# Attention scores of two heads in the two halves of TensorE: 64 rows for each head in place of 96 and 128 shared rows

## What is computed

```python
def attention(x):                       # x: 4 x 512 x 256
    q, k, v = split(x @ w_qkv.T + b_qkv)
    q, k = rope(q), rope(k)
    attn = einsum('bhqd,bhkd->bhqk', q, k) * 16 ** -0.5
    attn = softmax(where(causal, -inf, attn))
    return einsum('bhqk,bhkd->bhqd', attn, v) @ w_out.T + b_out

def ffn(x):
    hidden = silu(x @ W1.T) * (x @ W3.T)          # 1024 wide
    return fwht(hidden) @ W2.T

x = x + layernorm(attention(layernorm(x)))
x = x + layernorm(ffn(layernorm(x)))
```

## Time and profile before

| | us |
|---|---|
| median of 3 executions (501.43 to 504.0) | 502.22 |
| the profiled execution, whole | 503.94 |
| its span, first to last instruction | 502.2 |
| TensorE matmuls busy | 415.0 (83%) |
| TensorE weight loads busy | 343.4 (68%) |
| VectorE busy | 281.3 (56%) |
| ScalarE busy | 210.2 (42%) |
| GpSimd busy | 161.4 (32%) |

### The profile page before, as it was taken

How to read it: one execution, slowest core, us unless ns; L and a number is a source line. 1 busy time by engine, 2 the same in 40 slices (tenths; PEclk the granted TensorE clock), 3 DMA queues, 4 the chain that set the end, 5 groups by cost and what they waited for, 6 DMA issues and landing times.

```text
span 502.2 us, 7871 instructions
## 1 busy us (share of the span) xinstructions
PE 415.0 (83%) x2880; PEld 343.4 (68%) x2880; DVE 281.3 (56%) x936; ACT 210.2 (42%) x302; POOL 161.4 (32%) x280
## 2 busy tenths in 40 slices
PE   0669587998689998988599988988699889858993
PEld 0559554657579976557499965566699775448992
DVE  7454688036847679246856686257566781173114
ACT  4435222872433317843422338723333249422222
POOL 3136000642512215624412227514222226321332
PEclk9999965799979999999789999999599999996996
DMA  7639900000298001100697002001982002000001
GB/s 216 222 110 185 205 5 1 1 3 0 84 208 153 20 1 40 44 1 1 139 193 133 1 1 84 1 1 42 169 162 49 2 0 85 1 1 1 1 0 43
DMA packets 31751, 32.76 MB, mean 65 GB/s; under 512 B 2400, under 2 KB 30816, under 8 KB 31712
## 3 DMA queue, kind: packets, MB, share of 16 engines
q1 hardware_dynamic: 31712, 32.25, 28.5%
HBM read 21.76 MB, written 10.49 MB: 64 GB/s over the span
## 4 chain that ended last, share of the span: by engine, by line
PE 61%; DVE 14%; issue 8%; ACT 7%; DMA 6%; SPq 2%; POOL 1%; DVEq 0%; ACTq 0%; POOLq 0%
PE ps L250 33%; PE ps L423 8%; PE ps L437 7%; PE ps L411 6%; ACT probs L623 5%; DVE masked_scores L879 3%; DMA qk_scratch<-qk_s 2%; DMA raw_bias<-in_b_out 2%; DMA q_t<-qk_scratch 2%; PE ps L465 1%; DVE qk_s L840 1%; DVE xy L941 1%; PE ps L383 1%; DVE stats_h L826 1%; SPq L285 1%
## 5 line engine op out<-in xcount | busy, mean ns | idle before, releaser
L879 DVE CUSTOM_DVE_ANT_0 masked_scores<-ps,mask_row 128x128 bf16<-128x128 f32 (+3 forms) x256 | 114.1, 488 | 46.2 <-PE ps L411 45.7
L250 PE MATMUL ps<-xt,w_s 128*128 128x256 f32 x768 | 112.9, 297 | 0.0
L250 PEld LDWEIGHTS ps<-xt,w_s 128*128 128x128 f32 x768 | 107.7, 205 | 0.5
L762 POOL TENSOR_TENSOR hid_s<-gate,hid_s 128x512 fp32r<-128x512 f32 x32 | 41.1, 1285 | 137.5 <-ACT hid_s L635 137.5
L411 PE MATMUL ps<-k_t,q_t 96*128 96x128 f32 (+3 forms) x256 | 74.7, 368 | 10.8 <-DMA q_t<-qk_scratch 5.3
L623 ACT ACTIVATE probs<-ps 128x1280 f32<-128x1280 f32 x64 | 76.6, 1246 | 12.1 <-PE ps L423 10.8
L423 PEld LDWEIGHTS ps<-q_t,k_t 128*128 128x128 f32 x256 | 45.5, 202 | 34.0 <-ACT probs L623 17.4
L423 PE MATMUL ps<-q_t,k_t 128*128 128x512 f32 (+3 forms) x256 | 57.8, 353 | 6.9 <-ACT probs L623 5.3
L411 PEld LDWEIGHTS ps<-k_t,q_t 96*128 96x128 f32 x256 | 44.2, 200 | 24.6 <-DVE maxima L879 17.1
L250 PE MATMUL ps<-w_s,hid_s 128*128 128x256 f32 x384 | 57.4, 287 | 2.5 <-POOL hid_s L762 2.5
L250 PEld LDWEIGHTS ps<-w_s,hid_s 128*128 128x128 f32 x384 | 52.7, 193 | 3.7 <-POOL hid_s L762 2.9
(11 more groups left out here) (99 smaller groups left out, 481.5 us busy)
## 6 DMA issues: line engine op xcount, KB each, us to landing
qk_scratch<-qk_s SPq DMA_DIRECT2D x16, 512.0 KB, 5.7
k_t<-qk_scratch SPq DMA_DIRECT2D x48, 128.0 KB, 4.4
q_t<-qk_scratch SPq DMA_DIRECT2D x24, 256.0 KB, 7.2
xa<-in_x SPq DMA_DIRECT2D x4, 512.0 KB, 9.0
xy<-in_x SPq DMA_DIRECT2D x4, 512.0 KB, 3.5
out<-xy SPq DMA_DIRECT2D x8, 256.0 KB, 2.2
o_t<-in_w SPq DMA_DIRECT2D x1, 1024.0 KB, 10.8
raw_w<-in_w SPq DMA_DIRECT2D x1, 1024.0 KB, 8.3
```

Of the source, the lines that this page charges most:

```text
L250: ins = eng.matmul(o, lhs(i), rhs(j), start=first and n == 0, stop=last and n == 2, skip_group_check=skip)
L762: pool.tensor_tensor(hid_s[:, a % 2, 1, :], gate[:, a % 2, :], hid_s[:, a % 2, 0, :].bitcast(F32), ALU.subtract).then_inc(S["hid_l"], 1)
L879: ins = dve.tensor_tensor_reduce(masked_scores[:, SCORE_NO[n] % 2, i * keys:(i + 1) * keys], ps[:, banks[n], i * keys:(i + 1) * keys], mas ...
```

## The change

Each head of a pair now has 64 rows of its own (`BLOCK`), the even head rows 0 to 63 and the odd one rows 64 to 127: q high, q high, 16 rows of maxima (high and low part for the eight pairs), q low, against k high, k low, the selector, k high. `k_t` has a slice for every pair, with no rows of zeros. A matmul of the first pass takes the 64 rows of one head, and the two heads of a pair follow each other into two neighbouring banks. A score unit is now four, two, one and one **pairs**, in a pair of banks, so that there are 22 units and 4 turns in place of 44 and 4. All units that come within the feed-forward steps take banks 4 and 5 together.

The rows of maxima now take part in the first pass, so they have to be zero then: GpSimd zeroes both blocks of 16 rows of `q_t` after the attention of each sequence (`zero_rows`), and at the start. The turned maxima are copied in four pieces (even and odd head; first pair and the other seven), for the last query tile the odd ones by VectorE. The queries are fetched by six DMAs for each half, and the selector by four. `xt` has a buffer of its own, and the wait on `v_done` ahead of the fetch of queries is gone.

```diff
-QK_ROWS = 3 * 2 * HEAD
-MAX_ROWS = 2 * HEADS
+BLOCK = 4 * HEAD
+MAX_AT = 2 * HEAD
+Q_SLOTS = ((0, 0), (1, 0), (3, 1))
+K_SLOTS = ((0, 0), (1, 1), (3, 0))
+FETCHED = 16 * 2 * (len(Q_SLOTS) + len(K_SLOTS))
...
-    UNITS += [("scores", _qt, list(range(h, h + _n))) for h in range(0, HEADS, _n)]
+    UNITS += [("scores", _qt, list(range(a, a + _n))) for a in range(0, PAIRS, _n)]
...
-    UNITS.insert(min(_last + 5, len(UNITS)), ("turn", _qt, []))
+    UNITS.insert(min(_last + 3, len(UNITS)), ("turn", _qt, []))
...
-    banks = [4 + n % 2 for n in range(min(early, N_UNITS))]
-    order = [0, 1, 2, 3, 4, 5]
-    banks += [order[n % 6] for n in range(N_UNITS - len(banks))]
-    return banks[:-1] + [5]
+    banks = [4 for n in range(min(early, N_UNITS))]
+    order = [0, 2, 4]
+    banks += [order[n % 3] for n in range(N_UNITS - len(banks))]
+    return banks[:-1] + [4]
...
-UNITS_AFTER = [(0, 0, 0), (3, 2, 0), (1, 3, 0), (4, 1, 0), (4, 0, 0), (4, 5, 0), (5, 6, 0), (4, 2, 0), (0, 0, 3)]
+UNITS_AFTER = [(0, 0, 0), (2, 1, 0), (2, 1, 0), (2, 1, 0), (2, 1, 0), (2, 1, 0), (2, 2, 0), (2, 2, 0), (0, 0, 1)]
 STEPS, EARLY_UNITS = feed_forward_steps(UNITS_AFTER)
 STEPS_LAST, _ = feed_forward_steps(None)
 UNIT_BANKS = unit_banks(EARLY_UNITS)
-FIRST_UNIT_BANKS = [4 + n % 4 for n in range(N_UNITS - 1)] + [5]
+FIRST_UNIT_BANKS = [4 + 2 * (n % 2) for n in range(N_UNITS - 1)] + [4]
 PROBS = 10
-FIRST_SELECTOR = [None, 0, 2, 9]
-FIRST_TRANSFORM = [-1, -1, -1, -1, -1, 4, 8, 13]
-FIRST_W2_PARTS = [14, 19]
+FIRST_TRANSFORM = [-1, -1, -1, -1, -1, 2, 4, 7]
+FIRST_W2_PARTS = [8, 11]
...
         q_t = sb("q_t", [P, PAIRS, TOKENS], F32R)
-        k_t = sb("k_t", [P, HEADS, TOKENS], F32R)
-        xt = q_t[:, 0:4, :].rearrange("p (s c) t -> p s c t", s=2)
+        k_t = sb("k_t", [P, PAIRS, TOKENS], F32R)
+        xt = sb("xt", [P, 2, CH, TOKENS], F32R)
+        sel = sb("sel", [P, PAIRS])
...
-                    for j, ks in enumerate((0, 1, 0)):
+                    for slot, ks in K_SLOTS:
                         kp = scratch[ks, DIM:2 * DIM, c].rearrange("(a e p) t -> e p a t", e=2, p=HEAD)
                         for e in range(2):
-                            dst = k_words[32 * j + HEAD * e:32 * j + HEAD * e + HEAD, :, c]
-                            sp.dma_start(dst.rearrange("p (a e) t -> p e a t", e=2)[:, e, :, :], kp[e])\
+                            row = BLOCK * e + HEAD * slot
+                            sp.dma_start(k_words[row:row + HEAD, :, c], kp[e])\
                               .then_inc(S["qk_in" if half == 0 else "qk_in_late"], 16)
 
                 def fetch_q(half):
                     c = halves(half)
-                    for j, qs in enumerate((0, 0, 1)):
-                        sp.dma_start(q_words[32 * j:32 * j + 32, :, c],
-                                     scratch[qs, 0:DIM, c].rearrange("(a p) t -> p a t", p=32))\
-                          .then_inc(S["qk_in" if half == 0 else "qk_in_late"], 16)
+                    for slot, qs in Q_SLOTS:
+                        qp = scratch[qs, 0:DIM, c].rearrange("(a e p) t -> e p a t", e=2, p=HEAD)
+                        for e in range(2):
+                            row = BLOCK * e + HEAD * slot
+                            sp.dma_start(q_words[row:row + HEAD, :, c], qp[e])\
+                              .then_inc(S["qk_in" if half == 0 else "qk_in_late"], 16)
 
                 send(0)
                 fetch_k(0)
-                sp.wait_ge(S["v_done"], b * TILES + TILES)
...
-            sp.dma_start(sel[QK_ROWS:P, :], selector).then_inc(S["selector_in"], 16)
+            for e in range(2):
+                for half in range(2):
+                    row = BLOCK * e + MAX_AT + PAIRS * half
+                    sp.dma_start(sel[row:row + PAIRS, :], selector[HEADS * half:HEADS * half + PAIRS, 0:PAIRS])\
+                      .then_inc(S["selector_in"], 16)
...
-                        pe.wait_ge(S["rows_in"], 2 * (b * TILES + UNITS[before[-1]][1] + 1))
+                        pe.wait_ge(S["rows_even"], 2 * (b * TILES + UNITS[before[-1]][1] + 1))
+                        pe.wait_ge(S["rows_odd"], 2 * (b * TILES + UNITS[before[-1]][1] + 1))
...
-                for i, h in enumerate(heads):
-                    ins = pe.matmul(o[:, i * keys:(i + 1) * keys], q_t[0:QK_ROWS, h // 2, qt * P:qt * P + P],
-                                    k_t[0:QK_ROWS, h, 0:keys], start=(i == 0), stop=(i == len(heads) - 1),
-                                    skip_group_check=True)
+                for i, a in enumerate(pairs):
+                    for e in range(2):
+                        rows = slice(BLOCK * e, BLOCK * e + BLOCK)
+                        ins = pe.matmul(ps[:, banks[n] + e, i * keys:(i + 1) * keys], q_t[rows, a, qt * P:qt * P + P],
+                                        k_t[rows, a, 0:keys], start=(i == 0), stop=(i == len(pairs) - 1),
+                                        skip_group_check=True)
...
+                rows = slice(BLOCK * (h % 2), BLOCK * (h % 2) + BLOCK)
                 if h >= 2:
                     pe.wait_ge(S["exp_done"], b * HEADS + h - 1)
                 for kt in range(TILES):
                     col = 3 * (h % 2) * 512 + KEY_COL[kt]
                     n = TOKENS - kt * P
-                    ins = pe.matmul(ps[:, col // 512, col % 512:col % 512 + n], k_t[:, h, kt * P:kt * P + P],
-                                    q_t[:, h // 2, kt * P:TOKENS], start=(kt != 3), stop=(kt != 1), skip_group_check=True)
+                    ins = pe.matmul(ps[:, col // 512, col % 512:col % 512 + n], k_t[rows, h // 2, kt * P:kt * P + P],
+                                    q_t[rows, h // 2, kt * P:TOKENS], start=(kt != 3), stop=(kt != 1), skip_group_check=True)
...
-                    for first, pairs in ((0, 1), (1, PAIRS - 1)):
-                        act.activation(q_t[QK_ROWS:P, first:first + pairs, qt * P:qt * P + P],
-                                       ps[0:MAX_ROWS, banks[n], 0:P].unsqueeze(1).broadcast_to([MAX_ROWS, pairs, P]),
-                                       ACT.Copy).then_inc(S["rows_in"], 1)
-                elif heads[-1] == HEADS - 1:
+                    for first, count in ((0, 1), (1, PAIRS - 1)):
+                        for e, done in ((0, "rows_even"), (1, "rows_odd")):
+                            if e == 0 or qt < TILES - 1:
+                                row = BLOCK * e + MAX_AT
+                                act.activation(q_t[row:row + 2 * PAIRS, first:first + count, qt * P:qt * P + P],
+                                               ps[MAX_AT * e:MAX_AT * e + 2 * PAIRS, banks[n], 0:P].unsqueeze(1)
+                                               .broadcast_to([2 * PAIRS, count, P]), ACT.Copy).then_inc(S[done], 1)
...
+            def zero_rows(b):
+
+                pool.wait_ge(S["st_done"], (b + 1) * HEADS)
+                pool.wait_ge(S["masked"], (b + 1) * HEADS)
+                for e in range(2):
+                    row = BLOCK * e + MAX_AT
+                    pool.memset(q_t[row:row + 2 * PAIRS, :, :].bitcast(F32), 0.0).then_inc(S["rows_zeroed"], 1)
+                    pool.wait_ge(S["rows_zeroed"], 2 * b + e + 1)
...
+                if order is MIX:
+                    zero_rows(b)
...
+                    if qt == TILES - 1:
+                        dve.wait_ge(S["max_turned"], b * TILES + qt + 1)
+                        row = BLOCK + MAX_AT
+                        for first, count in ((0, 1), (1, PAIRS - 1)):
+                            dve.tensor_copy(q_t[row:row + 2 * PAIRS, first:first + count, qt * P:qt * P + P],
+                                            ps[MAX_AT:MAX_AT + 2 * PAIRS, banks[n], 0:P].unsqueeze(1)
+                                            .broadcast_to([2 * PAIRS, count, P])).then_inc(S["rows_odd"], 1)
...
-                for i, h in enumerate(heads):
-                    ins = dve.tensor_tensor_reduce(masked_scores[:, SCORE_NO[n] % 2, i * keys:(i + 1) * keys], ps[:, banks[n], i * keys:(i + 1) * keys],
-                                                   mask_row[:, TOKENS - keys:], 1.0, -3e38, ALU.add, ALU.max,
-                                                   maxima[:, qt % 2, h:h + 1])
+                for e in range(2):
+                    for i, a in enumerate(pairs):
+                        c = slice(i * keys, (i + 1) * keys)
+                        ins = dve.tensor_tensor_reduce(masked_scores[:, SCORE_NO[n] % 2, e, c], ps[:, banks[n] + e, c],
+                                                       mask_row[:, TOKENS - keys:], 1.0, -3e38, ALU.add, ALU.max,
+                                                       maxima[:, qt % 2, e, a:a + 1])
```

72 lines of the change are left out of this document (41 added, 31 removed).

## The result

The changed kernel takes **603.35 us** (599.83 to 605.15, 4 executions) against 502.33 us (501.43 to 504.0, 4 executions): a ratio of 1.1998, 95% interval 1.1935 to 1.2061. It is 101 us slower. I had predicted 517 us, in a range of 509 to 533. The direction was right; the loss is seven times the one that I worked out.

What follows compares the result with a forecast made beforehand. TensorE's queue was taken to bound the feed-forward stages, VectorE the last part of the start. +4.0 us for three stages (12) plus 2.7 at the start, on a 502.2 us span, gave 517 us; own range 511 to 525, whole range 509 to 533.

Steps and rivals of the forecast that it cites:

- what costs nothing: List of parts taken as free: GpSimd's zeroing, the added query fetches, copies of odd maxima, the dropped wait, the attention.
- My rival for the attention: Attention: loading 64 rows of the other half ahead hides 0.19 us for 10 heads, four times: -7.6, 509; chance 0.08.
- A lower granted clock: TensorE: a clock below 0.96, from the added waits, would make the kernel slower still; no size given.
- Changes of shape: Feed-forward stages: changing between whole array and halves exposes 0.16 us each, 5.4 us three times: +16, 533 us; chance 0.20.
- The circle of the single buffer: Feed-forward units: each waits for matmuls and reductions of the one directly ahead; 2.72, 2.05, 1.52, 1.84 us for 128 to 512 keys.
- The turns: Feed-forward stages: after three turns the next unit waits for two sets of ScalarE copies, 2.45 us each, so 7.35.
- The tail: End of a feed-forward stage: the last unit stands behind the last `down`, 4.8 us until the attention.
- The start: Start: three more selector DMAs +1.4 us, units behind a turn waiting for copies +0.8 and +0.5; together +2.7.
- The queries of the later sequences: Three more fetches in each half, 1.4 us of issue, counted as hidden; a first unit waiting for them would be wrong.
- The waits for the maxima: Feed-forward stages: TensorE's waits for the maxima should rise by about 7 us in each.
- the 5.3 us per stage saved: Three feed-forward stages: score pairs sharing the array take 5.3 us off TensorE's queue, which turn into waiting.
- my lower bound: Feed-forward stages: a pair at the price of one matmul gives 48.6 us, +2.4 three times, +1.4 at the start: 511.

Runs made afterwards that it cites:

- experiment 1: Changed kernel with the attention's second pass (scores) on all 128 rows in place of 64: 557.38 us, ratio 1.1102 to the kernel before.
- experiment 2: Kernel before with the attention's second pass on rows 64 to 127 only: 552.75 us, ratio 1.1018.
- experiment 3: Kernel before with the second pass on rows 0 to 95 (511.55 us, ratio 1.0203) or rows 0 to 79 (ratio 1.0482).
- Experiment 6: Kernel before with the first pass on rows 0 to 63 in place of 0 to 95: 538.56 us, ratio 1.075.
- experiment 5: Changed kernel with the second pass of a pair's two heads interleaved matmul by matmul: 585.57 us, ratio 1.1677 to the kernel before.
- experiment 7: Changed kernel, second pass on all 128 rows, one 128-row first-pass matmul per pair in feed-forward stages: 543.84 us, ratio 1.0848 to the kernel before.
- experiment 9: Changed kernel with queries fetched by four DMAs for each half in place of six: 600.75 us, ratio 1.1964 to the kernel before.

## Why the prediction was wrong in size

**The step that failed** is the last sentence on what costs nothing: "In the attention every head still has the same 1280 columns and changes the shape of tile as often; I take nothing." Columns and changes were counted rightly. That the clock would stay where it was I had not even named as a condition; it went from 1.00 to between 0.54 and 0.56. It cost 51 us of span; experiments 1 and 2 show the same loss from both sides (46 us taken away, 50 us made), and 3 its dependence on rows. My rival for the attention had the wrong sign. "A lower granted clock" stood there as a remark, put down to waits; in the attention it came with hardly any (matmuls busy for 40.20 of 41.00 us).

**Changes of shape** had 0.20 as a rival with 0.16 us for each. Experiment 6 shows 0.19, and there it is exposed: its stages grow from 46.2 to 57.2 us. The units of 384 keys are where it bites: 188.67 - 188.30 = 0.37 us for a pair and 190.29 - 188.67 = 1.62 us for twelve matmuls (1.44 before), so 1.99 us between these units in place of 1.67, over eight units +2.35 us. The rival was right that a change costs, and the forecast, which had nothing for it, was not; whether the next matmul waits for the end of the last, as the rival has it, no run shows.

**The circle of the single buffer** was sized well: 5.07 us for two units of 128 keys (5.44 predicted), 8.35 for four of 256 (8.20), 11.61 for six of 512 (11.04; mostly 1.91 us each where I had 1.84). The gate's product stood between two units' reductions in places and was not always covered.

**The turns** were mis-sized: 3.27, 2.82 and 2.86 us, sum 8.95, where I had 7.35. ScalarE in the first of them, with the unit that follows at 184.08:

```profile
180.89 0.60 ACT L646 ACTIVATE gate<-ps 128x512 f32<-128x512 f32 x1 [2.99 <-PE ps L253]
181.51 2.42 ACT L663 ACTIVATE q_t<-ps 16x128 fp32r<-16x128 f32 x4
```

A copy of 16 rows is no cheaper than one of 32, four take 2.42 us and not 2.14, and ahead of them stood an activation of the gate, which I had not looked for.

**The tail**, 4.8 predicted, is 228.02 - 221.30 = 6.72: 1.42 of the difference are the last twelve `down` at the lower clock, behind the waits for the maxima. Altogether such a stage is 56.4 us in place of my 50.2: +2.35 in the units of 384 keys, +1.6 in the turns, +1.9 in the tail and +0.35 in the other units. It is 59.7 in the one whose first 9 us had the lower clock. That one followed the longest wait for queries of the three, 3.61 us; in experiments 1, 5 and 7 too the stages behind waits of 3.4 us and more had granted clocks of 0.87 to 0.94, but in experiment 9 two stages behind 2.5 and 2.0 us had 0.91 and 0.89, so the cause stays open.

**The start** took +8.0 and not +2.7. SyncE's queue there:

```profile
38.02 4.01 SPq L297 DMA_DIRECT2D q_t<-qk_scratch  x6
...
52.98 2.80 SPq L297 DMA_DIRECT2D q_t<-qk_scratch  x6
```

The late queries arrive 3.65 us later (units wait until 64.41, before until 60.76), and the units and turns behind them take 29.0 us in place of 24.7. Of the 3.65, 2.3 are there when SyncE ends its issues (55.78 in place of 53.47); the rest is open. The clock is not what makes the 29.0: it is 0.56 there, and was 0.57. I had taken VectorE as fed; it is busy for 20.6 of the 29.0 us, where it was for 21.3 of 24.7. The first unit starts only 0.4 us later than before, so the 1.4 us for the issues of the selector can't be seen.

**The queries of the later sequences** I had called hidden. The first unit waits 2.6, 3.6 and 2.1 us for them: that was listed among what would prove me wrong, and it did. These 8.3 us, of which the kernel before had none, make up the +7.8 from the attentions to the first units. Experiment 9 does not settle how much of them comes from the three more DMAs.

**The waits for the maxima** were to rise by about 7 us in each such stage. In the three stages TensorE waits 4.0, 3.4 and 4.4 us for them where it waited 1.6, 1.8 and 2.3, so 2 us more each: the direction was right, the size was not. More than half of the growth over the whole kernel (3.6 to 18.8 us in the score matmuls) lies in the start.

**Right** were: that two halves share the array (I took 0.05 us for the second matmul; experiment 5 shows none that can be measured); that the 5.3 us per stage saved would not be seen; the waits of 1.1 to 1.5 us for ScalarE behind the turns; the 2.5 us idle between the last `down` and the attention; and that GpSimd's zeroing is hidden. GpSimd ahead of the first rotary product of a `mix`, to set against the earlier trace rows:

```profile
129.45 7.07 POOL L800 MEMSET q_t<- 16x4096 f32 x2
138.60 1.85 POOL L778 TENSOR_TENSOR rot_s<-qk_b,rope_t 128x256 f32<-128x256 f32 x2 [2.08 <-ACT qk_b L630]
```

7.07 us, and still 2.08 idle behind it.

**The sum.** Of 99.5 us: 51 the attention, by its clock (46.8 of them are gone in the trace of experiment 1, where the clock is 0.80 to 0.94); 33.6 the feed-forward stages, of which I had 12; 8 the start, of which I had 2.7; 7.8 from the attention to the first unit, of which I had nothing; and 0.9 comes back at the end. Of the 33.6, 15.4 are gone in experiment 7, without changes of shape and second heads; 18.2 stay, 5.1 to 6.6 us for each stage, where my lower bound, which had the same schedule, gave +2.4. How these 18.2 divide among the single buffer, the turns, the tail and the clock was not tested one by one.
